# Seven gather stages of a graph network: row gathers written out one by one into the resident array, instead of a loop over four slots

## The reference

```
h = jnp.maximum(_layernorm(x, axis=-1), 0.0)
x = x + _L0_gnn_ref(h, edge_index, ...)      # GCN, 2 layers
...
x = x + _L1_gnn_ref(h, edge_index, ...)      # SAGE, 2 layers
...
x = x + _L2_gnn_ref(h, edge_attr_16, ...)    # 3 layers, edge terms, layer norms
...
x = x + _L3_gnn_ref(h, edge_index, ...)      # GAT, 4 layers
# inside a layer, e.g. GCN:
msgs = norm[:, None] * xw[src]
out = jax.ops.segment_sum(msgs, dst, num_segments=n_nodes)
```

## Time and profile before

| | us |
|---|---|
| median of 3 runs | 7403.93 (7402.09 to 7414.38) |
| profiled execution | 7404.41, its span 7402.6 |
| the seven stages, first gather of C1 to first gather of GA | 2337.3 to 5157.1 |
| POOL busy | 3662.5 (49% of the span) |
| PE, DVE, ACT busy | 5017.4, 3865.3, 3026.6 |

### The profile page before, as it was taken

One profiled execution on the slowest core, in us unless ns is written; L12 is line 12 of the kernel. 1 busy time (PEld: TensorE's weight loads), 2 busy tenths in 40 slices (PEclk: granted clock), 3 DMA queues, 4 the chain that ended last, 5 costly groups with the idle time before them and its releaser, 6 DMA issues. The chain is left out here.

```text
span 7402.6 us, 131992 instructions
## 1 busy us (share of the span) xinstructions
PE 5017.4 (68%) x28362; PEld 3879.2 (52%) x28362; DVE 3865.3 (52%) x13753; ACT 3026.6 (41%) x7457; POOL 3662.5 (49%) x4925
## 2 busy tenths in 40 slices
PE   4777777777777987799778898765056066075077
PEld 3555555555555666566667777664055055064066
DVE  5555555555555457633566676775054054064076
ACT  3555555555554333344446665554022022022043
POOL 2333333333333555555555565333755745745756
PEclk9999999999998985599889999777588588588555
DMA  3444444444443336544563333333223223223233
GB/s 93 136 138 136 137 136 137 135 136 135 136 137 111 104 110 177 149 125 124 163 188 95 94 99 94 102 102 91 53 70 92 53 73 89 53 76 87 54 92 94
DMA packets 1077945, 815.46 MB, mean 110 GB/s; under 512 B 103820, under 2 KB 937170, under 8 KB 1077880
## 3 DMA queue, kind: packets, MB, share of 16 engines
q1 hardware_dynamic: 983800, 650.27, 29.1%
q0 software_dynamic: 94080, 164.48, 9.2%
HBM read 359.28 MB, written 459.01 MB: 111 GB/s over the span
## 5 line engine op out<-in xcount | busy, mean ns | idle before, releaser
L807 POOL DMA_INDIRECT M<-table,idx_slot x1372 | 1397.0, 1018 | 1194.0 <-PE PS L1367 470.1
L1367 PE MATMUL PS<-CR,LO 1*128 1x128 f32 (+3 forms) x4312 | 1069.7, 334 | 155.2 <-ACT CR L1663 155.2
L1367 PEld LDWEIGHTS PS<-CR,LO 1*128 1x128 f32 (+1 forms) x4312 | 779.5, 225 | 278.1 <-ACT CR L1663 189.1
L827 POOL DMA_INDIRECT G<-table,idx_all x784 | 739.8, 944 | 307.9 <-issue 237.7
L1663 ACT ACTIVATE CR<-PS 65x128 f32<-65x128 f32 (+2 forms) x1274 | 341.1, 268 | 1263.6 <-PE PS L1367 1248.0
L751 POOL DMA_INDIRECT M<-in_x,idx_slot x196 | 197.5, 1008 | 1049.6 <-ACT GN L1663 999.2
L1364 PE MATMUL PS<-ident,ES 128*98 128x128 f32 x16 | 4.3, 422 | 1003.9 <-DVE ES L426 1003.9
L1367 PE MATMUL PS<-G,S 128*128 (+2 forms) x2744 | 625.9, 314 | 0.0
L1367 PEld LDWEIGHTS PS<-WX,G 128*128 128x128 f32 x3136 | 406.4, 198 | 303.5 <-DVE G L1081 243.3
L426 DVE COPY ES<-G 128x392 f32<-128x392 f32 x4 | 2.1, 526 | 1016.5 <-DMA G<-table,idx_all 1016.5
L1364 PEld LDWEIGHTS PS<-ident,ES 128*98 128x98 f32 x16 | 2.6, 192 | 1004.9 <-issue 1004.8
(11 more groups left out here) (300 smaller groups left out, 12066.7 us busy)
## 6 DMA issues: line engine op xcount, KB each, us to landing
table<-G SPq DMA_DIRECT2D x392, 260.0 KB, 2.1
table<-G SPq DMA_DIRECT2D x392, 256.0 KB, 2.6
table<-RO SPq DMA_DIRECT2D x245, 256.0 KB
table<-RO SPq DMA_DIRECT2D x196, 260.0 KB
OWN<-table SPq DMA_DIRECT2D x196, 260.0 KB
XIN<-xrows SPq DMA_DIRECT2D x196, 256.0 KB
OWN<-table SPq DMA_DIRECT2D x147, 256.0 KB
xrows<-RB SPq DMA_DIRECT2D x147, 256.0 KB
```

Source lines behind the costliest of these rows:

```text
L807: g.indirect_dma_start(M[:, j, 0:w], None, table, bass.IndirectOffsetOnAxis(ap=idx_slot[:, at + j:at + j + 1], axis=0)).then_inc(gat[j].se ...
L827: g.indirect_dma_start(G[:, t, :], None, TAB[s], bass.IndirectOffsetOnAxis(ap=idx_all[:, t:t + 1], axis=0)).then_inc(gat[t % 4].sem, 16)
L1367: return nc.tensor.matmul(o, l, r, start=start, stop=stop)
```

## The change

The code of the seven stages' gathers becomes that of the attention stages: no loop, no copy of indices, no slot; 196 gathers a stage, each into its tile of `G`, in the order in which they are read. Only one wait stays: a gather waits for the landing of the one four before it, since the four semaphores `gat0` to `gat3` are taken in turn. The readers (PE's `tile`, DVE's `messages`) address `G` by the quad's number; `messages` writes its product over the gathered row, and `MP` goes. `M` is now a second name of `XIN` for the plain stage. `m_free` goes, and `FS` is packed closer.

```
@@ gathers, on POOL
-            def gather_quad(s, table, idx, w, n, half):
-                Q4 = n * (-4) + 4 * LAST
-                for j in range(4):
-                    pool.wait_ge(gat[j].sem, gat[j].at(s, n) - 16)
-                at = 4 * half
-                g.tensor_copy(idx_slot[:, at:at + 4], idx[:, ds(Q4, 4)]).then_inc(idxed.sem, 1)
-                for j in (3, 2, 1, 0):
-                    free = mprod if KINDS[s] in ("LA", "LB") else m_free
-                    used = (free.sem, free.last(s, n, f"t{j}"))
-                    alone(pool, used, *([(idxed.sem, idxed.at(s, n, "slots"))] if j == 3 else []))
-                    g.indirect_dma_start(M[:, j, 0:w], None, table,
-                                         bass.IndirectOffsetOnAxis(ap=idx_slot[:, at + j:at + j + 1], axis=0)
-                                         ).then_inc(gat[j].sem, 16)
...
+                idx, w = idx_l2 if kind in ("LA", "LB") else idx_all, GW if kind in ATTENDED else D
+                for t in reversed(range(T)):
+                    if kind not in ATTENDED:
+                        pool.wait_ge(gat[t % 4].sem, gat[t % 4].at(s, LAST - t // 4))
+                    g.indirect_dma_start(G[:, t, 0:w], None, TAB[s],
+                                         bass.IndirectOffsetOnAxis(ap=idx[:, t:t + 1], axis=0)
+                                         ).then_inc(gat[t % 4].sem, 16)
@@ messages, on DVE (LA, LB)
-                    v.scalar_tensor_tensor(MP[:, 4 * h + j, :], M[:, j, 0:D], wl2[:, ds(n * (-4) + (4 * LAST + j), 1)],
-                                           bank(5)[:, j, :], ALU.mult, ALU.add).then_inc(mprod.sem, 1)
+                    t = n * (-4) + (4 * LAST + j)
+                    row = G[:, ds(t, 1), 0:D]
+                    v.scalar_tensor_tensor(row, row, wl2[:, ds(t, 1)], bank(5)[:, j:j + 1, :],
+                                           ALU.mult, ALU.add).then_inc(mprod.sem, 1)
@@ tile, on PE
                 def rows_of(i):
-                    if kind in ATTENDED:
-                        return G[:, ds(n * (-4) + (4 * LAST + i), 1), :].rearrange("p t c -> p (t c)")
                     if kind in ("LA", "LB"):
                         pe.wait_ge(mprod.sem, mprod.at(s, n, f"t{i}"))
-                        return MP[:, 4 * h + i, :]
-                    pe.wait_ge(gat[i].sem, gat[i].at(s, n, "rows"))
-                    return M[:, i, 0:D]
+                    elif kind not in ATTENDED:
+                        pe.wait_ge(gat[i].sem, gat[i].at(s, n, "rows"))
+                    return G[:, ds(n * (-4) + (4 * LAST + i), 1), 0:w].rearrange("p t c -> p (t c)")
```

More of the change, by code:

```diff
@@ L149, in gnn_program @@
         PT = sb("PT", [P, 4, T])
-        M = sb("M", [P, 4, GW])
         idx_slot = sb("idx_slot", [P, 8], i32)
@@ L157, in gnn_program @@
         CR = sb("CR", [P, 2, GW])
-        FS = sb("FS", [P, 2, 3, 160])
+        FS = sb("FS", [P, 2, 3 * FIRSTS + 96])
         relK = sb("relK", [P, T])
@@ L162, in gnn_program @@
         XIN = sb("XIN", [P, 4, D])
+        M = XIN
         U = sb("U", [P, 4, D])
@@ L214, in gnn_program @@
         node_val, node_src = (lend(2 * ROOM + 10000 + k * 2 * T, T, 2) for k in (0, 1))
-        MP = lend(2 * ROOM + 11000, 8, D)
         e_rest = lend(2 * ROOM + 9300 + 512, 2, 4 * ED)
@@ L295, in steps @@
             return Steps(sem(name), order, by, start)
-        idxed = steps("idxed", {k: ("slots",) for k in KINDS if k not in ("GA", "GZ")})
+        idxed = steps("idxed", {"X": ("slots",)})
         gat = [steps(f"gat{j}", {k: ("rows",) for k in KINDS}, 16) for j in range(4)]
-        m_free = steps("m_free", {k: four for k in ("C1", "C2", "S1", "S2")}, 1, 4)
         sel = steps("sel", {k: four for k in AGG})
@@ L585, in plain @@
                     sp.wait_ge(gat[j].sem, gat[j].at(0, m, "rows"))
-                sp.dma_start(quad_rows(XR[0], m), M[:, :, 0:D]).then_inc(st_x.sem, 16)
+                sp.dma_start(quad_rows(XR[0], m), M[:, :, :]).then_inc(st_x.sem, 16)
                 keep_norm(m, 1, 2)
@@ L707, in _ @@
             g.memset(CR[:, :, :], 0.0)
-            g.memset(FS[:, :, :, :], 0.0).then_inc(m_free.sem, 4)
-            g.memset(M[:, :, :], 0.0).then_inc(agg.sem, 8)
+            g.memset(FS[:, :, :], 0.0).then_inc(agg.sem, 8)
             g.memset(den[:, :, :], 0.0).then_inc(mprod.sem, 4)
@@ L750, in beside_plain @@
                 for j in range(4):
-                    g.indirect_dma_start(M[:, j, 0:D], None, x,
+                    g.indirect_dma_start(M[:, j, :], None, x,
                                          bass.IndirectOffsetOnAxis(ap=idx_slot[:, 4 + j:5 + j], axis=0)
@@ L822, in _ @@
                 stage_stored(pool, s - 1)
+                idx, w = idx_l2 if kind in ("LA", "LB") else idx_all, GW if kind in ATTENDED else D
[5 more added lines that the diff above has]
+                                         ).then_inc(gat[t % 4].sem, 16)
                 if kind not in ATTENDED:
-                    gathers(s, TAB[s], idx_l2 if kind in ("LA", "LB") else idx_all, D)
                     continue
[L826 to L829, removed]
                 pool.wait_ge(m_v.sem, m_v.at(0, ATTENTION.index(s), "weights"))
@@ L1094, in x_sums @@
                 for j in range(4):
-                    i = v.bn_stats(stat[:, j, :], M[:, j, 0:D])
+                    i = v.bn_stats(stat[:, j, :], M[:, j, :])
                 x_step(m, i, "stats")
@@ L1177, in select @@
                         rel3 = rel[:, ds(Q4 + 1, 3)]
+                        firsts = FS[:, h, :].rearrange("p (i c) -> p i c", c=FIRSTS + 32)[:, :, 0]
                         if weight is None:
-                            v.tensor_scalar(FS[:, h, :, 0], rel3, 0.0, None, ALU.is_equal)
+                            v.tensor_scalar(firsts, rel3, 0.0, None, ALU.is_equal)
                         else:
-                            v.scalar_tensor_tensor(FS[:, h, :, 0], rel3, 0.0, weight[:, ds(Q4 + 1, 3)],
+                            v.scalar_tensor_tensor(firsts, rel3, 0.0, weight[:, ds(Q4 + 1, 3)],
                                                    ALU.is_equal, ALU.mult)
@@ L1501, in tile @@
                 if j == 3 and kind not in CHAINED:
-                    firsts = FS[:, h, :, :].rearrange("p i c -> p (i c)")
                     for i in (3, 2, 1):
-                        at = P * (i - 1)
-                        r = mm(first_sums(kind, w), firsts[:, at:at + FIRSTS], rows_of(i), i == 3, i == 1)
+                        at = FIRSTS * (i - 1)
+                        r = mm(first_sums(kind, w), FS[:, h, at:at + FIRSTS], rows_of(i), i == 3, i == 1)
                     r.then_inc(rsum.sem, 1)
-                main = mm(A, S[:, slot, :], rows_of(j), True, False)
-                if kind in m_free.order and kind not in ATTENDED:
-                    main.then_inc(m_free.sem, 1)
+                mm(A, S[:, slot, :], rows_of(j), True, False)
                 if between:
@@ L1742, in plain @@
                 for j in range(4):
-                    i = f(GN[:, j, :], M[:, j, 0:D], ACT.Relu, scale=rs[:, j:j + 1], bias=nb[:, j:j + 1])
+                    i = f(GN[:, j, :], M[:, j, :], ACT.Relu, scale=rs[:, j:j + 1], bias=nb[:, j:j + 1])
                 i.then_inc(ad.sem, 1)
```

## The result

The changed kernel took **7290.3 us** (median of 4, 7283.3 to 7301.8) against 7403.0 (median of 4) of the kernel before on the same chip: ratio 0.9847, 95% interval 0.983 to 0.9864, 113 us less. Forecast were 7301 us and a range of 7235 to 7360. That chip turned out to be the kind one. The later runs were on four others, which the record numbers 11, 5, 3 and 6: the kernel before took 7544 to 7609 us there, and the changed kernel, timed again on chip 5, was 19% slower.

The account below looks back on a forecast made before the run. No engine was full; a loop through several, with PE and POOL waiting over the slots, set the period. Gains of 28 (C2), 50 (S2), 19 (LA) and 6 (starts), 103 us, took 7404.4 to 7301 us; range 7235 to 7360.

Parts of the forecast that it names:

- PE's 51 us of register instructions: Seven stages: four more PE register instructions a quad, 51 us if none were hidden; taken as 0, behind queued matmuls.
- rival D: PE's added register instructions show in the stages that PE paces: 29 us less gain, 7330 us; chance 0.06.
- (b): C2: the load into single `XIN` waits for its reader `RB`; period 6.6 to 7.1 us, 6.95 taken, gain 28.
- (c): C2: `OWN`'s load stands behind the table store, 2.14 us behind `U`; with PE early it goes out early too.
- 3.53 + landing + 4.90 over two quads: S2: loop of table store, `OWN` load (3.03 to 3.5 us) and norm; 6.0 us a quad taken, gain 50 us.
- half of the 19.2: LA, twice: half of DVE's 19.2 us of gather waits returns, 9.6 us each, 19 together.
- Rival C: C2, S2, LA: every wait for gathers comes back whole, 192 us, 7212 us in all; chance 0.13.
- floor (a): C2: DVE's own chain from one combine to the next, 6.34 us a quad without any wait.
- rival B: C2, S2: more gathers in flight make loads land later, taking the gathers' place; gain 48 us, 7356; chance 0.15.
- 3.51: C2: time in which an `XIN` load lands after its issue, 3.51 us or less.
- Rival E: POOL becomes the bound: unspaced gathers beside DVE's work last up to 1462 ns each; 7428 us, slower; chance 0.04.
- The one wait left ... is met: POOL: the gather four before, 5.0 us earlier, has landed if gathers land within about 4 us of their start.

Follow-up runs that it names:

- two-buffer kernel: The changed kernel with second buffers of both `XIN` and `OWN` in C2 and S2: 9018 us on chip 11, ratio 1.193 to the kernel before.

## Why the prediction was right, and where it was not

On the first chip its steps held, one by one. C1, S1: no gain in the loop, measured 7.67 before and after. PE's 51 us of register instructions were hidden, as its first-GA rows had said (rival D out). C2: the load into the single `XIN` (b) was the next limit, 6.6 to 7.1; it measured 6.81, its term 37 for 29. The number is a mean of two regimes that the sum did not have: 6.92 beside gathers, 6.46 behind them. That this mean lies so near (b) is in part luck: DVE waits for `XIN` in 30 quads of 49 only, 13.8 us in all, and most of the gain is the wait for `OWN`, which (c) had seen go. S2: 3.53 + landing + 4.90 over two quads; the term was 51 and measured 46, since `OWN` landed in 3.9 beside gathers and not in 3.0 to 3.5. LA: half of the 19.2, 0.2 us a quad, measured 0.20. LB gave 3.7 for 0.8, small and not looked into. The 9.7 us outside the seven stages lie in code that the change leaves alone, and the four runs of the kernel differ by 18.5 us; they are no proof of anything. Rival C fell at floor (a), which the two-buffer kernel reached at 6.37; rival B's later landing came in S2, by 0.6 us, and not in C2. (The 3.51 us that the forecast had for a load of C2 is one load; the stage's median was 3.81.)

Rival E was priced for the wrong cause. Gathers last 965 ns and not 1430, and DVE's work kept its length; the Trainium skill ("SBUF — State Buffer", section "Who interferes with whom") has GpSimd and a DVE instruction in a two-port mode block each other at a shared port. What these runs show is another thing, since what came late were signals, PE's nearly all of them. What failed on the later chips is a step that the prediction counted as plain gain: "The one wait left ... is met", so that POOL never pauses. There an unpaused POOL holds the signals of PE, and some of DVE, back by 10 to 30 us and more, each stage on chip 5 is 161 to 241 us longer than in the kernel before on chip 3 (the 248 that its gathers take, or most of them), and the forecast's sign is wrong. That it was tested on the one chip of five where this costs nothing was luck. The first chip's trace could not have told: neither kernel has a stall over 0.5 us there.

Not settled: what in the chip the signals and the gathers share, and why one chip shows no stall where four do. The chip is the difference that the record names; no run went back to the first one, so something else about the first result's conditions is not excluded. Nor is the profiler: every time on record has a profiled span beside it, and the later chips' traces lack up to a fourth of the increments' records, so no run shows how long these kernels take unprofiled. Which of the two buffers carries C2's 0.43 was not tried beside gathers on a chip where hand-offs are on time.

## What to carry to other kernels

A ring of slots may be too short for one stage and long enough for the next; ask of each stage whether the reader ever waits, and then what the next loop is (here a load into a single buffer), since that gave the new period to about 2%. On the later chips two quads of run-ahead were enough for C2, four were worse, and gathers written out without any bound took away POOL's pauses, on which those chips depend; whether two quads would have kept the whole gain on the first chip was not tried. Time such a change on more than one chip before believing it. And look for a late signal in the waiter's start, not in the semaphore's records, of which a trace can lack a fifth.

## What the runs showed of the hardware that was not expected

While POOL issues indirect gathers without a pause, signals of PE to ACT and DVE, and a few of DVE to PE, can arrive 10 to 70 us late on some chips (71 stalls of ACT and DVE over 8 us in seven stages on chip 5) and on time on another (none over 0.5 us). A wait for the landing of the gather one or two before brings them back to time (none and one over 1 us, chip 3). The gathers' own increments are not held back: each of the four semaphores goes on rising about every 5 us. The delay outlasts the gathers: 10 to 22 us behind the last of 196 unpaused ones PE's signals to DVE are still 3.4 to 4.8 us late, on all four later chips.
